# Transposing and masking the last step's probabilities ahead of the scores and the merge in steps 8 to 60

## The reference

```python
x = x + _L0_attn_ref(_layernorm(x, axis=-1), L0_attn_wq, L0_attn_wk, L0_attn_wv, L0_attn_wo)
x = x + _L0_ffn_ref(_layernorm(x, axis=-1), L0_ffn_w1, L0_ffn_b1, L0_ffn_w2, L0_ffn_b2)

q = _apply_rotary(split_heads(hidden_states @ wq), cos, sin)      # k alike, v without rotation
valid = (k_pos > q_pos - WINDOW) & (k_pos <= q_pos)
attn = jnp.einsum('bhqd,bhkd->bhqk', q, k) * scale
attn = jnp.where(valid, attn, neg)
attn = jax.nn.softmax(attn, axis=-1)
out = jnp.einsum('bhqk,bhkd->bhqd', attn, v)
return out.transpose(0, 2, 1, 3).reshape(Bsz, Ln, NUM_HEADS * HEAD_DIM) @ wo
```

## Time and profile before

| | us |
|---|---|
| median of 3 runs | 355.96 |
| lowest and highest | 354.94, 357.53 |
| the profiled execution | 354.97 |
| its span in the trace | 352.9 |
| TensorE matmul busy | 340.2 |
| TensorE weight load busy | 314.6 |
| VectorE busy | 263.5 |
| GpSimd busy | 224.0 |
| ScalarE busy | 208.1 |

### The profile page before, as it was taken

How to read it: one execution, slowest core, us unless ns; L and a number is a source line. 1 busy time by engine, 2 the same in 40 slices (tenths; PEclk the granted TensorE clock), 3 DMA queues, 4 the chain that set the end, 5 groups by cost and what they waited for, 6 DMA issues and landing times.

```text
span 352.9 us, 6925 instructions
## 1 busy us (share of the span) xinstructions
PE 340.2 (96%) x2410; PEld 314.6 (89%) x2410; DVE 263.5 (75%) x607; ACT 208.1 (59%) x626; POOL 224.0 (63%) x182
## 2 busy tenths in 40 slices
PE   8987999999999999999999999999999999899896
PEld 7776879999999999999999999999999999878886
DVE  4875885678767876788789986777677767968581
ACT  2335775776685557655675576556665566375180
POOL 2327888767586759799879887776777567311300
PEclk9999999999999999999999999999999999999999
DMA  7935565443333333333332333333322231000001
GB/s 206 240 85 156 146 180 154 119 102 87 81 85 86 89 90 90 92 90 84 73 88 73 82 95 84 88 90 91 89 62 59 62 89 32 0 3 0 32 30 59
DMA packets 29025, 31.25 MB, mean 89 GB/s; under 512 B 3392, under 2 KB 20288, under 8 KB 28992
## 3 DMA queue, kind: packets, MB, share of 16 engines
q1 hardware_dynamic: 28992, 30.82, 34.2%
HBM read 12.98 MB, written 1.05 MB: 40 GB/s over the span
## 4 chain that ended last, share of the span: by engine, by line
PE 83%; DVE 6%; DMA 2%; POOL 2%; ACT 2%; issue 2%; SPq 1%; DVEq 0%; POOLq 0%
PE PR L389 22%; PE OT L468 13%; PE VO L406 13%; PE SC L441 12%; PE VO L423 11%; PE PT L452 4%; PE PR L496 2%; PE SC L496 2%; DMA v_raw<-in_wv 2%; PE VO L515 1%; PE SC L515 1%; POOL turn L962 1%; DVE gT_lo L819 1%; DMA swapped<-by_sin 1%; DVE xnorm L715 1%
## 5 line engine op out<-in xcount | busy, mean ns | idle before, releaser
L967 POOL TENSOR_TENSOR gT_lo<-turn,gT_hi 128x512 fp32r<-128x512 f32 x62 | 82.3, 1327 | 40.5 <-ACT gT_hi L599 40.4
L962 POOL TENSOR_TENSOR turn<-turn,swapped 128x512 f32<-128x512 f32 x62 | 80.3, 1294 | 30.6 <-DMA swapped<-by_sin 25.4
L604 ACT ACTIVATE probs<-SC,negmax 128x128 f32<-128x128 f32 x128 | 45.9, 364 | 58.3 <-DVE negmax L766 58.2
L611 ACT ACTIVATE probs<-probs,rinv 128x128 f32<-128x128 f32 x128 | 44.5, 395 | 36.6 <-DVE rinv L771 36.6
L468 PE MATMUL OT<-probsT,v_sb 128*128 128x128 f32 x450 | 60.2, 275 | 1.6 <-DVE gT_lo L784 1.6
L468 PEld LDWEIGHTS OT<-probsT,v_sb 128*128 128x128 f32 x450 | 55.3, 192 | 2.7 <-DVE probsT L777 2.7
L389 PE MATMUL PR<-xT_hi,qk_lo 128*128 128x512 f32 x128 | 55.5, 434 | 1.4 <-DVE xT_lo L723 1.4
L763 DVE COPY_PREDICATED SC<-in_prev_sb,SC 128x256 f32<-128x256 int32 x48 | 20.5, 428 | 41.7 <-PE SC L441 41.6
L389 PE MATMUL PR<-xT_hi,qk_hi 128*128 128x512 f32 x128 | 50.5, 394 | 0.0
L389 PE MATMUL PR<-xT_lo,qk_hi 128*128 128x512 f32 x128 | 50.0, 391 | 0.0
L777 DVE TENSOR_TENSOR probsT<-PT,mask_sb 128x512 f32<-128x512 f32 x64 | 43.5, 680 | 1.2 <-PE PT L452 1.2
(11 more groups left out here) (118 smaller groups left out, 846.5 us busy)
## 6 DMA issues: line engine op xcount, KB each, us to landing
swapped<-by_sin SPq DMA_DIRECT2D x128, 128.0 KB, 2.3
qk_raw<-in_wq SPq DMA_DIRECT2D x16, 128.0 KB, 2.6
qk_raw<-in_wk SPq DMA_DIRECT2D x16, 128.0 KB, 2.3
v_raw<-in_wv SPq DMA_DIRECT2D x8, 256.0 KB, 3.0
o_raw<-in_wo SPq DMA_DIRECT2D x8, 256.0 KB, 3.0
xres<-in_x SPq DMA_DIRECT2D x4, 256.0 KB, 3.4
w_raw<-in_w1t SPq DMA_DIRECT2D x4, 256.0 KB, 3.3
w_raw<-in_w2t SPq DMA_DIRECT2D x4, 256.0 KB, 3.0
```

What stands on the lines that cost most here:

```text
L604: nc.scalar.activation(probs[n % 2][:, i], SC[n % 2][:, i * 256 + P:(i + 1) * 256], ACT.Exp, bias=negmax[:, n % 2, i:i + 1], accum_out=row ...
L611: last = nc.scalar.activation(probs[n % 2][:, i], probs[n % 2][:, i], ACT.Copy, scale=rinv[:, n % 2, i:i + 1])
L962: tt(turn[m % 4][:], turn[m % 4][:], swapped[m % 2][:], ALU.add).then_inc(rot_done, 1)
L967: tt(rot_lo(head, c % 2)[:, half_of(c)], turn[m % 4][:], rot_hi(head, c % 2)[:, half_of(c)].bitcast(F32), ALU.subtract).then_inc(rotlo_don ...
```

## The change

In steps 8 to 60 `transpose_probs(n - 1)` is issued on TensorE ahead of `scores(n)`, and `mask_pt(n - 1)` on VectorE ahead of `merge(n)`. In the other steps both stay behind. At step 20 `means_of_abs` and `mean_sums` are moved with them, ahead of the scores and of the merge, so that their order to the transposes and the mask stays. No instruction is added or taken away, and no wait of any instruction is changed.

```diff
--- before.py
+++ after.py
@@ -232,6 +232,10 @@
 
             return slice((c // 2) * HALF, (c // 2 + 1) * HALF)
 
+        def turned_first(n):
+
+            return 8 <= n < STEPS - 3
+
         MEANS_AT = 20
         BELOW_AT = 25
         PIECES = 8
@@ -529,13 +533,15 @@
             transpose_x(0, 1)
             project(2, KD)
             for n in range(STEPS):
+                if n == MEANS_AT:
+                    means_of_abs()
+                if turned_first(n):
+                    transpose_probs(n - 1)
                 scores(n)
                 if n == 0:
                     project(3)
                     fill(0)
-                if n == MEANS_AT:
-                    means_of_abs()
-                if n > 0:
+                if n > 0 and not turned_first(n):
                     transpose_probs(n - 1)
                 if n + 4 < CHUNKS:
                     project(n + 4)
@@ -864,11 +870,13 @@
                     moments(1, 0)
                 if n == STEPS - 1:
                     ot_lo(n - 2)
-                merge(n)
-                if n > 0:
+                if turned_first(n):
                     mask_pt(n - 1)
                 if n == MEANS_AT:
                     mean_sums()
+                merge(n)
+                if n > 0 and not turned_first(n):
+                    mask_pt(n - 1)
                 if 1 < n < STEPS - 1:
                     ot_lo(n - 2)
                 if n == 0:
```

## The result

| | before | changed |
|---|---|---|
| median of 19 runs, us | 356.61 | 354.54 |
| lowest to highest | 354.53 to 360.92 | 352.72 to 356.41 |
| span of the profiled execution | 352.9 | 351.2 |

The ratio is 0.9952, with a 95% interval of 0.9933 to 0.9972: some 1.7 us less. That lies in the forecast range and under the 1% that was called no change. It is still three times the forecast gain of 0.5 us, and the forecast ratio (0.9985) lies outside the interval. So the direction and the range held, and the size is what the experiments are about.

A forecast was written before the change was run, and what follows sets the result against it. The prediction took TensorE's own dense stream as the bound. Its terms, -0.3 (junction) + 0.17 (step 40) - 0.38 (step 60) = -0.5 us, took the median from 355.96 to 355.4 us, range 353.6 to 357.7.

The forecast's parts named there:

- TensorE's stream is the bound, and nothing waits at a junction: Steps 8 to 60: TensorE busy 242.6 of 243 us, so reordering gains only where it removes a TensorE wait.
- The range: Median time after the change, whole kernel: 353.6 to 357.7 us, with the forecast at 355.4.
- the lower bound of the costs: Whole kernel: junction down to -1.1 and the step 60 stall wholly gone (-0.5) give 354.3 us.
- the junction: Transposes no longer directly behind the scores matmuls, 53 steps: gain of 0 to 1.1 us, 0.3 taken.
- step 40: Front of step 40: TensorE waits for the scaling, late after step 38's 1.77 us ternary; +0.17 us, bounds 0 to 1.4.
- The pair costs the same in its new place: Two transposes on TensorE, between weigh_v and scores: they cost 0.22 us a step, as behind the scores.
- The new order on VectorE: Step 51 as model: mask ends before scores, merge 0.22 late, scaling 0.12 earlier, margins 0.52 and 0.29 us.
- The rival of small waits at the front: Late merge reaches the scaling, so 13 short steps wait 0.11 us each; 357.7 us at most, chance 14%.
- Step 60, -0.38: Stall ahead of weigh_v in step 60 falls from 0.52 to 0.14 us, as ot_lo comes 0.38 earlier.
- The rival of over 1% slower: Transposes' load cannot be done ahead at the front: 0.11 us in each of 53 steps, 361.8 us, chance 8%.
- The rival of over 1% faster: Transposes no longer cut the stream between scores and projection: over 0.067 us a step, 351.9 at 0.07, chance 5%.

The follow-up runs named there:

- e0_after: The changed kernel itself, run again as yardstick against the kernel before: ratio 0.9953, steps 8 to 59 in 236.95 us.
- e11_after_again: The changed kernel run once more as yardstick against the kernel before: ratio 0.9966, steps 8 to 59 in 236.95 us.
- e4_only60: Kernel before with both moves (transposes, mask) in step 60 alone: ratio 0.9992 to the kernel before, step 60 in 3.47 us.
- e8_ot_lo_early: Changed kernel, but VectorE takes ot_lo(n - 2) ahead of merge in steps 60 and 61: ratio 0.9996 to the kernel before.
- e10_fill_idle: Changed kernel, but one add_out goes ahead of the reciprocal in steps 60 and 61, and ot_lo(59) ahead of merge(61): ratio 0.9970 to the kernel before.

## Why the prediction was right, and where it was not

- **TensorE's stream is the bound, and nothing waits at a junction.** Right. It is why the whole effect is 0.5%.
- **The range.** It held, and by its width: the measured terms add to -1.56 (1.19 and 0.37), which is the lower bound of the costs (354.3, or -1.6) and not the -0.5 of the forecast. The two errors, 0.9 in the junction and 0.17 in step 40, lie on the same side.
- **The pair costs the same in its new place; the junction gives 0 to 1.1 us, take 0.3.** This is the term that was mis-sized: it measured 1.19 us over 52 steps, 0.023 each, just past the far bound. I had looked for it in the intervals next to the pair, and all that lies outside the projection and the fill is 0.007. Two thirds sit in the projection and the fill, whose intervals I took as given. The reason I leaned on, that the change of type costs, also falls: the count of changes is not what the time follows.
- **The new order on VectorE.** Right to 0.03 us in each term: mask ahead of the scores, merge 0.22 late, the scaling some 0.12 early, margins 0.49 and 0.28. The kernel with TensorE's half alone shows that these margins were needed: without the move on VectorE the short steps wait. The rival of small waits at the front is thus what happens to half of the change, at 0.064 us for each short step where it priced 0.11, and not to the whole.
- **Step 40, +0.17.** It did not come, and that is luck. The `ternary` of step 38 took 0.74 us instead of 1.77. VectorE's row in the changed kernel:

```profile
196.54 0.74 DVE L814 SCALAR_TENSOR_TENSOR w_sb<-w_raw,thr,w_sb 128x512 fp32r<-128x512 f32 x1
```

POOL's, in the same kernel:

```profile
195.16 1.29 POOL L957 TENSOR_TENSOR qk_lo<-qk_raw,qk_hi 128x512 fp32r<-128x512 f32 x1
196.76 1.69 POOL L975 TENSOR_TENSOR gT_lo<-turn,gT_hi 128x512 fp32r<-128x512 f32 x1 [0.31 <-ACT gT_hi L605]
```

  It now starts in a gap of POOL (196.45 to 196.76), and the POOL instruction that comes into it is the one drawn out, 1.69 against its usual 1.3. The Trainium skill ("SBUF — State Buffer", section "Who interferes with whom") says that the one that starts first holds the ports and the other is blocked; both traces agree with that in who is drawn out.

  The new order doesn't keep the ternaries out of collisions. Which of them is long differs between executions of one kernel: the longest of the eight took 1.16 us in this execution of the changed kernel, 1.63 in e0_after and 1.36 in e11_after_again, and the one of step 38 took 1.77 in the kernel before but 1.13 in e4_only60, which has the same order there. So the 1.77 was one execution's value, not a property of the step. The mechanism of the term is real, as e8_ot_lo_early shows, whose steps up to 59 are those of the changed kernel. VectorE, ScalarE and the front load of step 42 in it:

```profile
206.89 1.90 DVE L814 SCALAR_TENSOR_TENSOR w_sb<-w_raw,thr,w_sb 128x512 fp32r<-128x512 f32 x1
...
211.40 0.70 ACT L617 ACTIVATE probs<-probs,rinv 128x128 f32<-128x128 f32 x2
...
212.15 0.20 PEld L456 LDWEIGHTS PT<-ident_sb,probs 128*128 128x128 f32 x2
```

  The scaling ends at 212.10, the load follows 0.05 later, and step 42 is 0.06 us longer than in the changed kernel. A ternary of 1.74 in the same place (e10_fill_idle) costs nothing. No run shows 1.77 in step 38 under the new order, so the 0.17 itself stays untested.
- **Step 60, -0.38.** Right. It measured -0.37, and moving only this step gives the same. TensorE's rows for it in the changed kernel (compare):

```profile
294.55 0.28 PE L427 MATMUL VO<-o_hi,gT_hi 128*128 128x256 f32 x1
294.82 0.57 PE L472 MATMUL OT<-probsT,v_sb 128*128 128x128 f32 x3
```

And VectorE's:

```profile
294.26 0.42 DVE L790 TENSOR_TENSOR gT_lo<-OT,gT_hi 128x256 fp32r<-128x256 f32 x1
```

  The interval ahead of `weigh_v` is 0.27 where 0.64 stood, so 0.15 of stall is left; 0.14 was forecast.
- **The rival of over 1% slower** (loads that cannot be done ahead): the front load of step 52 starts at 256.01, 0.11 ahead of its matmul at 256.12, and no step pays for it. Refuted.
- **The rival of over 1% faster** named the right place, scores and projection, but asked for 0.067 a step where there are 0.023.

## What to carry to other kernels

Where one engine's stream is dense, a reordering on it is worth its waits; find them in the waits view and at the odd steps of the loop, where buffers or work differ (here one step gave 0.37 us, predicted to 0.01). When an instruction moves to the front of an engine's list, compute when its input comes under the new order of the other engines too: the two halves of this change were worth nothing apart (steps 8 to 60 together: -0.05 and +0.21 us). A collision that one trace shows in one step need not be there in the next execution, so price it by how often it comes. And price a move by the whole step from start to start, not by the intervals beside it.

## What the runs showed of the hardware

- A pair of fp32 transposes directly ahead of six fp32r products of 512 columns makes a step 0.022 to 0.030 us longer than the same pair at the three other places that were tried, and most of it appears in later matmuls. A single transpose there costs nearly as much. The sum of steps 8 to 59 repeats to 0.005 us between executions and chips (236.951, 236.951 and 236.955 for the changed kernel), which is what makes such an effect visible at all.
- The same VectorE instruction, `ternary`, took between 0.74 and 1.90 us in these traces, and its length in one step differs between executions of one kernel.
- Executions differ at their ends. TensorE's granted clock, as the mean of a stretch, fell in the last part of some of them; the profiled execution with only TensorE's order changed lost 1.6 us there against the changed kernel (44.24 to 42.63 us from step 63 to the last matmul). Its row for that part in the windows view:

```profile
315.00:350.00 35.00, 33.55 (x212) 30.42 (x211) 24.11 (x49) 15.06 (x26) 3.81 (x5) 0.95 0.07 23
```

That of the changed kernel:

```profile
315.00:350.00 35.00, 31.45 (x211) 28.48 (x209) 23.16 (x48) 14.38 (x25) 3.82 (x5) 1.00 0.09 30
```

  This, and up to 1.9 us of difference ahead of step 8 between the traces, is a part of the spread of the timed runs, which is 3.7 us for the changed kernel and 6.4 for the one before. A comparison by whole executions needs many of them to see 0.4 us.
